# A transformer block on one core: first batch's norm on VectorE, ScalarE's steps interleaved, four part slots, and the last batch's chain in halves

## The chip, the cores and the metric

The kernel runs on one core of a Trainium2 chip. Five engines work side by side and meet at semaphores: TensorE (PE in the rows) for matrix products and transposes, VectorE (DVE), ScalarE (ACT), GpSimd (POOL), and SyncE (SP), which here only issues DMA transfers. Each engine runs its own instructions strictly in order. The metric is the device time of one execution in microseconds (us); less is better.

## The reference

The input x has 4 batches of 512 tokens of 128 channels. A small conditioning vector c per batch gives six modulation rows. The block is attention and then a mixture of experts, each behind a layer norm with modulation:

```python
mod = (_silu(L0_c) @ L0_wmod).reshape(4, 6, 1, -1)
sa, ca, ga, sb, cb, gb = (mod[:, i] for i in range(6))
ga = (2 * (ga >= 0) - 1) * jnp.maximum(jnp.abs(ga), 0.25)      # gb likewise
h = _layernorm(x) * (1 + ca) + sa
x = x + ga * attention(h)        # 16 heads of 8; q = h Wd Wu + rope(h Wd Wr), k likewise; softmax
h = _layernorm(x) * (1 + cb) + sb
x = x + gb * experts(h)          # sigmoid gates; each of 8 experts takes its 512 best tokens of 2048,
                                 # gelu(ex W1 + b1) W2 + b2, times the gate, added back
```

## The kernel before

There are three stretches. In the **head**, each batch b is normed (`moments`, `rstd`, `normed_1`), turned by TensorE (`turn_x`), scaled and shifted to hT by ScalarE (`h_out`) and projected (`project_k`, `project_rest`). VectorE adds bias and rotation (`rotate_k`, `parts_k`); the sum of a batch's keys is kf (L799). Keys and queries are then split into three bfloat16 parts each: high (a rounded copy, ScalarE's `key_high` and `query_high`), middle (`key_mid`, `query_mid`, of the first difference) and low (the second difference). VectorE forms the key differences, GpSimd the query sum (`rotate_q`, `parts_q`: L392, L398) and differences (L401, L405). SyncE stores each part to DRAM (`store_parts`) and reads them back in another layout (`load_group`). The part buffers kp and qp have two slots, used by batches in turn, so the high part of batch 3 waits until the stores of batch 1 are done (semaphores w_k, w_q).

The **attention** works on 16 groups (4 batches by 4 groups of heads). For each group TensorE computes the scores for the row maxima (`max_unit`, 8 a group, L1188), VectorE reduces each to maxima (`maxima`, L839, a semaphore count each), GpSimd splits the maxima in parts (`max_parts`) and SyncE moves them beside the queries (`load_max`, L295); then TensorE computes the scores again (`exp_unit`), ScalarE takes the exponential and TensorE weighs the values (`weigh`). Maxima run two groups ahead of the exponentials, so those of groups 0 and 1, all 16, stand before the first `step`. Beside them TensorE does the value products (`project_v`) and three of the four modulation rows (`modrows`).

After the last group comes the **tail** of batch 3: copy of the output (`out_copy`, L667), transposes (`out_turn`, L1238), division by the row sums (`normed`, L824 and L828), transposes (`turn_a`), copy (`a_out`), output projection (`project`), residual and statistics (`residual`, L855), rstd on GpSimd (L512), norm (`normed_2`, L875), transposes (`turn_h`, L1273), scale and shift (`h2_out`, L890), gate products (`route_gates`, L1284), exponential and reciprocal (`gates_out`, `gates_in`, L899). Each step takes the whole batch of four tiles of 128 tokens. `keep_warm(1)` puts one unused product of 512 columns between. Then VectorE searches the gates' thresholds, GpSimd gathers the rows of each expert, and the experts run.

The order on every engine is written out by hand. On ScalarE in the head it is all norms and h first, and then the parts:

```python
            for b in range(1, NB):
                normed_1(b)
                h_out(b)
            act.wait_ge(s_bd, 1)
            for b in range(NB):
                ...
                key_high(b, u)
```

## Time and profile before

| what | us |
|---|---|
| median of 3 runs | 424.71 (424.31 to 425.78) |
| profiled execution, its own time | 423.78 |
| its span, first to last instruction | 422.0 |
| PE busy in the span | 313.6 (74%) |
| DVE busy | 270.2 (64%) |
| ACT busy | 205.7 (49%) |
| POOL busy | 180.6 (43%) |

The times in the profile count from the first instruction of the span. In a timeline row the bracket at the end says how long the engine had been idle and who ended it. A row that merges several instructions says so with x and their number.

### The profile page before, as it was taken

The page shows a single profiled execution, that of the slowest core. Times are in us where ns is not written, and L with a number is a line of the kernel's source. Part 1 is how long each engine was busy: PE and PEld are TensorE (multiplying, and loading weights), DVE is VectorE, ACT ScalarE, POOL GpSimd, SP SyncE. Part 2 cuts the span into 40 slices and gives each one's busy share as a digit, 9 for nine tenths or more (in the row PEclk, how much of TensorE's full clock was granted, in tenths as well). Part 3 has the DMA queues.
Part 4 walks back from the last instruction along what each step waited for, and adds up shares of the span by engine and source line. Part 5 has one row for each costly group of instructions (what it writes and reads, how often), then busy time and mean ns, then how long its engine had stood idle before and what let it go on. Part 6 is the DMA issues. An engine that isn't in the chain of part 4 may idle for free.

```text
span 422.0 us, 7330 instructions
## 1 busy us (share of the span) xinstructions
PE 313.6 (74%) x2326; PEld 148.7 (35%) x2326; DVE 270.2 (64%) x540; ACT 205.7 (49%) x394; POOL 180.6 (43%) x208
## 2 busy tenths in 40 slices
PE   4998375999999999999989984101378996690930
PEld 3533042323333333333335333100244764460630
DVE  4459878898999999999976934677642442220210
ACT  2654232888888889888886550100033242211200
POOL 5237541666611111111113713000086877788672
PEclk9999679999999999999999998555587999966895
DMA  8322861011111111111002300700023565544332
GB/s 241 86 101 84 299 227 39 7 43 40 40 40 41 40 39 38 39 38 43 26 4 83 97 0 25 206 0 0 2 66 115 121 145 117 112 83 79 28 28 19
DMA packets 34488, 30.39 MB, mean 72 GB/s; under 512 B 5280, under 2 KB 28704, under 8 KB 34464
## 3 DMA queue, kind: packets, MB, share of 16 engines
q1 hardware_dynamic: 28320, 23.65, 18.2%
q0 software_dynamic: 6144, 6.43, 9.1%
q8 instruction: 14, 0.23, 0.2%
q14 instruction: 10, 0.08, 0.1%
HBM read 18.27 MB, written 11.60 MB: 71 GB/s over the span
## 4 chain that ended last, share of the span: by engine, by line
PE 44%; DVE 18%; POOL 16%; issue 10%; DMA 5%; ACT 4%; ACTq 0%; DVEq 0%; SPq 0%; POOLq 0%
PE ps L1225 14%; POOL out L558 10%; PE ps L1188 8%; PE ps L1211 6%; DVE mx L839 5%; POOL ex L547 5%; DVE big L954 3%; PE ps L1426 2%; DMA out<-big,idx 2%; PE ps L1238 2%; ACT osb L667 2%; DVE KB L875 1%; PE ps L1455 1%; DMA k_parts<-big 1%; PE ps L1306 1%
## 5 line engine op out<-in xcount | busy, mean ns | idle before, releaser
L839 DVE TENSOR_REDUCE mx<-ps 128x2 f32<-128x1024 f32 x128 | 148.2, 1218 | 10.0 <-PE ps L1188 10.0
L690 ACT ACTIVATE big<-ps 128x512 f32<-128x512 f32 x256 | 139.3, 598 | 26.5 <-PE ps L1211 24.5
L1225 PE MATMUL ps<-big,VA 128*32 128x256 f32 (+1 forms) x960 | 80.1, 405 | 3.0 <-ACT osb L667 2.3
L1188 PE MATMUL ps<-KB,QB 48*128 48x512 bf16 x256 | 50.6, 397 | 12.1 <-DVE mx L839 10.6
L547 POOL DMA_INDIRECT ex<-rows,idx x32 | 34.3, 1073 | 51.4 <-DVE idx L1058 40.8
L1211 PE MATMUL ps<-QB,KB 51*128 51x512 bf16 x256 | 54.7, 382 | 1.7 <-ACT osb L667 1.1
L558 POOL DMA_INDIRECT out<-big,idx x32 | 50.4, 1574 | 13.1 <-issue 8.8
L736 ACT ACTIVATE big<-ps,b1c 128x512 f32<-128x512 f32 x32 | 22.0, 687 | 66.2 <-PE ps L1426 66.2
L427 POOL TENSOR_TENSOR VA<-Vall,bv_row 128x128 f32 (+1 forms) x16 | 7.3, 454 | 72.2 <-PE ps L1225 72.2
L1426 PE MATMUL ps<-big,w1s 128*128 128x512 f32 x64 | 35.8, 680 | 2.0 <-DVE big L1024 1.6
L1455 PEld LDWEIGHTS ps<-w2s,big 128*128 128x128 f32 x256 | 30.3, 196 | 6.5 <-issue 4.7
L1188 PEld LDWEIGHTS ps<-KB,QB 48*128 48x128 bf16 x256 | 12.1, 93 | 57.0 <-DVE mx L839 31.0
L1225 PEld LDWEIGHTS ps<-big,VA 128*32 128x32 f32 x960 | 19.3, 107 | 36.5 <-issue 34.7
L1455 PE MATMUL ps<-w2s,big 128*128 128x128 f32 x256 | 31.0, 280 | 0.9 <-ACT big L736 0.9
L1211 PEld LDWEIGHTS ps<-QB,KB 51*128 51x128 bf16 x256 | 21.9, 94 | 14.7 <-ACT big L690 5.3
L1024 DVE COPY big<-ps 128x512 f32<-128x512 f32 x8 | 5.5, 692 | 33.3 <-PE ps L1415 33.3
L1069 DVE TENSOR_TENSOR big<-ps,b2r 128x256 f32<-128x256 f32 x16 | 6.8, 424 | 30.8 <-PE ps L1455 30.8
L1400 PE MATMUL ps<-big,same_e 128*128 128x3 f16 x15 | 2.8, 186 | 24.5 <-DVE big L954 24.5
L1415 PE MATMUL ps<-ident,ex 128*128 128x128 f32 x32 | 6.4, 335 | 19.4 <-DMA ex<-rows,idx 19.4
L437 POOL CAST mxp<-mxn 16x128 bf16<-16x128 f32 x16 | 4.5, 279 | 37.5 <-ACT mxn L660 19.7
L727 ACT ACTIVATE big<-ps 16x64 f32<-16x64 f32 (+1 forms) x2 | 0.5, 267 | 40.3 <-PE ps L1437 40.3
L1426 PEld LDWEIGHTS ps<-big,w1s 128*128 128x128 f32 x64 | 12.3, 218 | 14.6 <-issue 9.6
(172 smaller groups left out, 413.9 us busy)
## 6 DMA issues: line engine op xcount, KB each, us to landing
KB<-k_parts SPq DMA_DIRECT2D x32, 96.0 KB
QB<-q_parts SPq DMA_DIRECT2D x32, 96.0 KB
w1s<-in_w SPq DMA_DIRECT2D x8, 256.0 KB, 2.8
w2s<-in_w SPq DMA_DIRECT2D x8, 256.0 KB, 3.0
k_parts<-big SPq DMA_DIRECT2D x4, 384.0 KB, 3.2
q_parts<-big SPq DMA_DIRECT2D x4, 384.0 KB, 4.5
QB<-mxp SPq DMA_DIRECT2D x96, 2.0 KB
rows<-rw SPq DMA_DIRECT2D x1, 1088.0 KB, 6.0
```

Of the source, the lines that this page charges most:

```text
L547: pool.indirect_dma_start(out=ex[:, e % 2, c, :], out_offset=None, in_=rows_dram, in_offset=bass.IndirectOffsetOnAxis(ap=idx[:, e, c:c + 1 ...
L558: pool.indirect_dma_start(out=out_rows, out_offset=bass.IndirectOffsetOnAxis(ap=idx[:, e, c:c + 1], axis=0), in_=ys[:, e % 2, c, :], in_of ...
L667: nc.scalar.activation(osb[:], ps[:, 6, :], ACT.Copy).then_inc(s_oe, 1)
L690: nc.scalar.activation(PT[:, u, 2 * i + half, kc, :], ps[:, EXP_BANKS[n], :], ACT.Exp, scale=SCALE).then_inc(s_ex, 1)
L736: nc.scalar.activation(hid[:, u, f, :], ps[:, 1 + f, :], ACT.Gelu, bias=bias).then_inc(s_gelu, 1)
L839: nc.vector.tensor_reduce(mx[:, u, :].rearrange("p (h a) -> p h a", h=2)[:, :, n], ps[:, max_bank(u, n):max_bank(u, n) + 2, :], AX.X, ALU.max,
L954: ins = nc.vector.tensor_scalar(ge3[:, j, :], sv, now[:, j:j + 1].bitcast(fp32), None, ALU.is_ge, ALU.add, accum_out=cnt3[:, j:j + 1])
L1188: ins = mm(ps[:, max_bank(u, n) + half, :], QB[rows, r, i, qc * 128:(qc + 1) * 128], KB[rows, r, i, :], start=True, stop=True)
L1211: mm(ps[:, EXP_BANKS[n], :], KB[rows, r, i, kc * 128:(kc + 1) * 128], QB[rows, r, i, :], start=True, stop=True).then_inc(s_sc, 1)
L1225: ins = mm(ps[32 * j:32 * j + 32, 6, cols], VA[:, u, kc, j, :], PT[:, u, j, kc, cols], start=kc == 0 and not cols.start, stop=kc == TC - 1 ...
L1426: mm(ps[:, 1 + f, :], w1s[:, u, f * 128:(f + 1) * 128], exT[:, u, :], start=True, stop=True).then_inc(s_up, 1)
L1455: ins = mm(ps[:, 5 + h, at * 128:(at + 1) * 128], hid[:, u, f, c * 128:(c + 1) * 128], w2s[:, u, f, :], start=f == 0, stop=f == FC - 1)
```

## The change

In the head, GpSimd fills `ones` first, and TensorE begins with sixteen products of that tile that nobody reads. The norm of batch 0 moves from ScalarE to VectorE (it then needs no nmr). ScalarE's copies of the weight product stand behind the first `h_out`, and its norms and h of the later batches stand between the part steps of batches 0 and 1. On TensorE the bias products move behind the transposes of batch 0 and the first row product behind the key products; `project_rest(1)` goes ahead of `turn_x(3)`; the row and value products beside the maxima are issued in halves, one between each two units. kp and qp have a slot for each of the four batches, so ScalarE waits for no store; SyncE stores batch 1 before it loads group 1, and so on. GpSimd's and VectorE's loops over batches are written out.

In the tail, the chain of the last batch is issued in two halves of two tiles, with a pair of PSUM banks at each step, and sixteen unused products of 256 columns take the place of `keep_warm(1)`. The aggregate of the statistics, the epsilon, rstd and the last reciprocal stay whole.

The diff, cut; parts left out of the halves have the same pattern as those shown:

```diff
+LAST_O, LAST_A, LAST_GATES = (2, 4), (3, 5), (1, 7)
...
-        kp, qp = view(2, 3, L, dt=bf16), view(2, 3, L, dt=bf16)
+        kp, qp = view(NB, 3, L, dt=bf16), view(NB, 3, L, dt=bf16)
...
-            store_parts(0, 0)
-
+            store_parts(0)
             sp.wait_ge(s_one, 1)
-            sp.wait_ge(w_k[0], 16 + 48)
-            sp.wait_ge(w_q[0], 16 + 48)
+            sp.wait_ge(w_k[0], 48)
+            sp.wait_ge(w_q[0], 48)
             load_group(0, 0)
+            store_parts(1)
             load_group(0, 1)
-            store_parts(1, 1)
-            store_parts(2, 0)
+            store_parts(2)
             load_group(0, 2)
-            store_parts(3, 1)
+            store_parts(3)
             load_max(0, 0)
             load_group(0, 3)
-            for u in range(2):
-                sp.wait_ge(w_k[u], 16 + 96)
-                sp.wait_ge(w_q[u], 16 + 96)
+            for b in range(1, NB):
+                sp.wait_ge(w_k[b], 48)
+                sp.wait_ge(w_q[b], 48)
...
-                sp.wait_ge(s_x2, b + 1)
+                sp.wait_ge(s_x2, b + 1 if b + 1 < NB else NB + 1)
...
-            for s_ in (*w_k, *w_q):
-                pool.sem_inc(s_, 16)
+            nc.gpsimd.memset(ones[:], 1.0).then_inc(s_ones, 1)
...
+            rotate_q(0)
+            rounded_q(0)
+            low_q(0)
+            rotate_q(1)
+            for b in range(1, NB):
+                rounded_q(b)
+                if b + 1 < NB:
                     rotate_q(b + 1)
...
+            act.wait_ge(s_modc, 2)
+            h_out(0)
             act.wait_ge(s_wc, 1)
             nc.scalar.activation(wc[:, 0:512], ps[:, 6, :], ACT.Copy)
             nc.scalar.activation(wc[:, 512:640], ps[:, 7, 0:128], ACT.Copy).then_inc(s_wce, 1)
-            act.wait_ge(s_modc, 2)
-            normed_1(0)
-            h_out(0)
+            normed_1(1)
             modrow_out(0)
-            for b in range(1, NB):
-                normed_1(b)
-                h_out(b)
+            h_out(1)
+            normed_1(2)
             act.wait_ge(s_bd, 1)
-            for b in range(NB):
-                u = b % 2
-                key_high(b, u)
+            key_high(0)
+            query_straight(0)
+            key_mid(0)
+            query_high(0)
+            h_out(2)
+            normed_1(3)
+            query_mid(0)
+            key_high(1)
+            query_straight(1)
+            key_mid(1)
+            h_out(3)
+            query_high(1)
+            for b in range(2, NB):
...
-            out_copy(15)
-
-
-            gates_out(3)
+            act.wait_ge(s_pv, NS)
+            act.wait_ge(s_ot, NS - 1)
+            for h in range(2):
+                cols = slice(h * L // 2, (h + 1) * L // 2)
+                nc.scalar.activation(osb[:, cols], ps[:, 6, cols], ACT.Copy).then_inc(s_oe, 1)
+            for h in range(2):
+                cols = slice((3 * TC + 2 * h) * NE, (3 * TC + 2 * h + 2) * NE)
+                act.wait_ge(s_gl, NB + h)
+                ins = nc.scalar.activation(ge[:, cols], ps[:, LAST_GATES[h], cols], ACT.Exp, scale=-1.0)
+            ins.then_inc(s_ge, 1)
...
+            dve.wait_ge(s_rstd, 1)
+            for n in range(TC):
+                ins = nc.vector.tensor_scalar(xn[:, n, :], X[:, n, :], mv[:, n, 0:1], rstd[:, n:n + 1],
+                                              ALU.subtract, ALU.mult)
+            ins.then_inc(s_xn, 1)
...
-            normed(15, LAST_TURN)
-            a_out(3)
-            residual(3)
-            normed_2(3)
-            h2_out(3)
+            for h in range(2):
+                cols = slice(8 * h, 8 * h + 8)
+                dve.wait_ge(s_ot, NS + h)
+                o = ps[:, LAST_O[h], 0:L // 2].rearrange("p (a d) -> p a d", d=32)
+                nc.vector.reciprocal(rs[:, cols].unsqueeze(2), o[:, :, HD:HD + 1]).then_inc(s_rs, 1)
...
+            dve.wait_ge(s_y, NB - 2)
+            for h in range(2):
+                dve.wait_ge(s_aT, NB + h)
+                nc.vector.tensor_copy(aT[:, 1, h * L // 2:(h + 1) * L // 2],
+                                      ps[:, LAST_A[h], 0:L // 2]).then_inc(s_aTe, 1)
+            for h in range(2):
+                rows = slice(3 * TC + 2 * h, 3 * TC + 2 * h + 2)
+                dve.wait_ge(s_y, NB + h)
+                nc.vector.tensor_tensor(x2[:, rows], ps[:, LAST_GATES[h], 0:2 * D].rearrange("p (c d) -> p c d", c=2),
+                                        X[:, rows, :], ALU.add).then_inc(s_x2, 1)
+                dve.wait_ge(s_x2, NB + h)
+                for n in range(rows.start, rows.stop):
+                    ins = nc.vector.bn_stats(stat2[:, n, :], x2[:, n, :])
+                ins.then_inc(s_st2, 1)
...
+            for c in range(TC):
+                n = 3 * TC + c
+                ins = nc.vector.tensor_scalar(xn2[:, 1, c, :], x2[:, n, :], mv2[:, n, 0:1], rstd2[:, n:n + 1],
+                                              ALU.subtract, ALU.mult)
+                if c % 2 == 1:
+                    ins.then_inc(s_xn2, 1)
...
+            warm_x = ones[:].bitcast(bf16)
+
+            def stay_warm(n):
+
+                for _ in range(n):
+                    mm(ps[:, 6, 0:256], warm_x[:, 0:128], warm_x, start=True, stop=True)
+
+            pe.wait_ge(s_ones, 1)
+            stay_warm(16)
...
             turn_x(0)
-            modrows(0, 1)
+            for j in range(4):
+                mm(ps[:, 5, j:j + 1], w_ct[:, j * D:(j + 1) * D], bcol[:, 0:1], start=True, stop=True)
+            mm(ps[:, 5, 128:256], bcol[:, 0:1].to_broadcast([128, 128]), w_ct[:, 4 * D:5 * D],
+               start=True, stop=True).then_inc(s_bias, 1)
             pe.wait_ge(l_wx, 16)
             project_k(0)
+            modrows(0, 1)
             turn_x(1)
             pe.wait_ge(s_wce, 1)
             pe.wait_ge(s_modc, 2)
...
             project_rest(0)
             turn_x(2)
             project_k(1)
+            project_rest(1)
             turn_x(3)
-            project_rest(1)
             project_k(2)
...
-                if n == 2:
-                    pe.wait_ge(s_qt, NB + 1)
-                    modrows(1, 6)
-                if n == 4:
-                    project_v(0)
-                if n == 6:
-                    project_v(1)
+                if n in (1, 2):
+                    modrow_half(1, n - 1)
+                if n in (3, 4):
+                    project_v(0, n - 3)
+                if n in (5, 6):
+                    project_v(1, n - 5)
                 if n == 7:
-                    pe.wait_ge(s_modr, 2)
-                    modrows(2, 6)
+                    modrow_half(2, 0)
...
+                if n == 0:
+                    modrow_half(2, 1)
+                if n in (1, 2):
+                    project_v(2, n - 1)
+                if n in (3, 4):
+                    project_v(3, n - 3)
+                if n in (5, 6):
+                    modrow_half(3, n - 5)
...
-            out_turn(15, LAST_TURN)
-            turn_a(3)
-            project(3)
-            keep_warm(1)
-            turn_h(3)
-            route_gates(3)
...
+            pe.wait_ge(s_x2, NB - 1)
+            pe.wait_ge(s_ge, NB - 1)
+            for h in range(2):
+                pe.wait_ge(s_aTe, NB + h)
+                for c in range(2):
+                    at = (2 * h + c) * 128
+                    ins = mm(ps[:, LAST_GATES[h], c * 128:(c + 1) * 128], aT[:, 1, at:at + 128], wo_g[:, 3, :],
+                             start=True, stop=True)
+                ins.then_inc(s_y, 1)
+            stay_warm(16)
+            for h in range(2):
+                pe.wait_ge(s_xn2, NB + h)
+                for c in range(2):
+                    ins = nc.tensor.transpose(ps[:, LAST_A[h], c * 128:(c + 1) * 128], xn2[:, 1, 2 * h + c, :], ident[:])
+                ins.then_inc(s_h2t, 1)
+            pe.wait_ge(s_x2, NB + 1)
+            for h in range(2):
+                pe.wait_ge(s_h2e, NB + h)
+                for c in range(2 * h, 2 * h + 2):
+                    n = 3 * TC + c
+                    ins = mm(ps[:, LAST_GATES[h], n * NE:(n + 1) * NE], h2T[:, 1, c * 128:(c + 1) * 128], wg[:],
+                             start=True, stop=True)
+                ins.then_inc(s_gl, 1)
```

## Rows read from the trace of the kernel before

**Rows 1.** The page: the granted clock of TensorE in 40 slices, and one group of instructions.
```profile
PEclk9999679999999999999999998555587999966895
...
L1069 DVE TENSOR_TENSOR big<-ps,b2r 128x256 f32<-128x256 f32 x16 | 6.8, 424 | 30.8 <-PE ps L1455 30.8
```

**Rows 2.** The chain that ended last: start us, length us, what.
```profile
44.95 4.74 DMA k_parts<-big
...
67.03 4.63 DVE mx L839 x4
...
305.78 1.96 POOL ex L547
```

**Rows 3.** Timeline of the first 30 us: start us, us, engine, line, operation, idle before.
```profile
4.37 0.20 POOL L379 MEMSET ones<- 128x128 f32 x1
...
5.46 1.87 PE L1099 MATMUL ps<-se,wmod 128*128 128x4 f32 x8 [5.46 <-DVE se L753]
...
7.15 1.04 POOL L385 TENSOR_TENSOR rstd<-var,mhalf 128x4 f32<-128x4 f32 x1 [2.58 <-DVE var L767]
...
9.10 0.64 PE L1104 MATMUL ps<-w_ct,wdT 128*128 128x128 f32 x2
...
12.33 0.28 DVE L781 TENSOR_TENSOR bv_row<-bv_row,ps 128x128 f32<-128x128 f32 x1
...
13.32 0.78 ACT L599 ACTIVATE big<-ps,modcol 128x512 f32<-128x512 f32 x1 [1.27 <-PE ps L1125]
...
18.30 0.75 DVE L787 SCALAR_TENSOR_TENSOR big<-ps,bcol,cos_t 128x512 f32<-128x512 f32 x1 [5.70 <-PE ps L1133]
...
20.48 0.75 DVE L799 SCALAR_TENSOR_TENSOR big<-ps,bcol,big 128x512 f32<-128x512 f32 x1
```

**Rows 4.** Timeline from 30 to 62 us.
```profile
30.17 0.75 DVE L799 SCALAR_TENSOR_TENSOR big<-ps,bcol,big 128x512 f32<-128x512 f32 x1
...
33.93 1.16 POOL L405 TENSOR_TENSOR big<-big 128x512 bf16<-128x512 f32 x1
...
43.54 0.61 PE L1188 MATMUL ps<-KB,QB 48*128 48x512 bf16 x4 [1.24 <-DMA QB<-q_parts]
...
44.50 0.75 DVE L799 SCALAR_TENSOR_TENSOR big<-ps,bcol,big 128x512 f32<-128x512 f32 x1
...
46.48 2.35 DVE L839 TENSOR_REDUCE mx<-ps 128x2 f32<-128x1024 f32 x2
...
54.46 0.61 PE L1188 MATMUL ps<-KB,QB 48*128 48x512 bf16 x2 [3.55 <-DVE mx L839]
...
55.00 2.08 PE L1152 MATMUL ps<-wc,big 128*128 128x128 f32 x8
...
57.66 3.49 DVE L839 TENSOR_REDUCE mx<-ps 128x2 f32<-128x1024 f32 x3 [1.32 <-PE ps L1188]
```

**Rows 5.** Timeline from 62 to 100 us.
```profile
62.03 1.16 PE L1152 MATMUL ps<-wc,big 128*128 128x128 f32 x8
...
63.86 4.07 SPq L295 DMA_DIRECT2D QB<-mxp  x6
```

**Rows 6.** Timeline from 237 to 269 us.
```profile
237.26 4.18 DVE L875 TENSOR_SCALAR KB<-X,mv,rstd 128x128 f32<-128x128 f32 x4 [0.73 <-POOL rw L518]
...
251.16 0.60 ACT L667 ACTIVATE osb<-ps 128x512 f32<-128x512 f32 x1 [1.19 <-PE ps L1225]
...
255.78 0.69 DVE L855 TENSOR_TENSOR X<-ps,X 128x512 f32<-128x512 f32 x1 [1.25 <-PE ps L1261]
...
259.13 1.12 DVE L875 TENSOR_SCALAR KB<-X,mv,rstd 128x128 f32<-128x128 f32 x4 [1.13 <-POOL rstd L512]
...
260.30 1.11 PE L1273 MATMUL ps<-ident,KB 128*128 128x128 f32 x4 [3.70 <-DVE KB L875]
...
262.32 1.88 PE L1284 MATMUL ps<-wg,h2T 128*128 128x8 f32 x8 [0.90 <-DVE h2T L890]
...
264.68 0.35 DVE L899 RECIPROCAL g_en<-ge 128x32 f32<-128x32 f32 x1
```

More of the change, by code:

```diff
@@ L195, in build @@
         s_qh, s_qr, s_qm, s_ql = (sem(n) for n in ("s_qh", "s_qr", "s_qm", "s_ql"))
-        w_k = [sem(f"w_k{u}") for u in range(2)]
-        w_q = [sem(f"w_q{u}") for u in range(2)]
+        w_k = [sem(f"w_k{b}") for b in range(NB)]
+        w_q = [sem(f"w_q{b}") for b in range(NB)]
         s_one = sem("s_one")
@@ L392, in rotate_q, with rounded_q @@
                 nc.gpsimd.tensor_tensor(qad[:], qcs[:], qss[:], ALU.add).then_inc(s_qad, 1)
-            def parts_q(b, u, more=True):
+            def rounded_q(b):
                 pool.wait_ge(s_qad, b + 2)
@@ L514, in rows_2 @@
             def rows_2(b):
-                pool.wait_ge(s_xn2, b + 1)
+                pool.wait_ge(s_xn2, b + 1 if b + 1 < NB else NB + 1)
                 rows = rw[:, b * TC:(b + 1) * TC, 0:D]
@@ L652, in _ @@
             values_out(1)
-            modrow_out(2)
             def max_out(s):
@@ L693, in _ @@
             max_out(0)
+            modrow_out(2)
             values_out(2)
@@ L903, in _ @@
             rotate_k(0)
-            with dve.Fori(0, NB // 2 - 1) as it:
-                parts_k(it * 2, 0)
-                parts_k(it * 2 + 1, 1)
-            parts_k(NB - 2, 0)
-            parts_k(NB - 1, 1, more=False)
+            for b in range(NB):
+                parts_k(b, more=b + 1 < NB)
             for n in range(3, 8):
@@ new lines, in _ @@
+            dve.wait_ge(s_st2, 2 * NB)
+            for n in range(3 * TC, 4 * TC):
+                ins = nc.vector.bn_aggr(mv2[:, n, :], stat2[:, n, :])
+            ins.then_inc(s_st2, 1)
+            dve.wait_ge(s_st2, 2 * NB + 1)
+            nc.vector.tensor_scalar_add(var2[:, 3 * TC:], mv2[:, 3 * TC:, 1], EPS).then_inc(s_v2, 1)
+            dve.wait_ge(s_r2, NB)
+            dve.wait_ge(s_xm2, NB - 2)
+            dve.wait_ge(s_h2t, NB - 2)
+            for c in range(TC):
[4 more added lines that the diff above has]
+                    ins.then_inc(s_xn2, 1)
@@ L943, in _ @@
+            dve.wait_ge(s_gl, NB - 2)
+            for h in range(2):
+                cols = slice(h * L // 2, (h + 1) * L // 2)
+                dve.wait_ge(s_h2t, NB + h)
+                nc.vector.tensor_scalar(h2T[:, 1, cols], ps[:, LAST_A[h], 0:L // 2], modcol[:, 3, 3:4], modcol[:, 2, 3:4],
+                                        ALU.mult, ALU.add).then_inc(s_h2e, 1)
             gates_in(3)
@@ L1104, in _ @@
             mm(ps[:, 7, 0:D], wdT[:], w_ct[:, 512:640], start=True, stop=True).then_inc(s_wc, 1)
-            for j in range(4):
-                mm(ps[:, 5, j:j + 1], w_ct[:, j * D:(j + 1) * D], bcol[:, 0:1], start=True, stop=True)
-            mm(ps[:, 5, 128:256], bcol[:, 0:1].to_broadcast([128, 128]), w_ct[:, 4 * D:5 * D],
-               start=True, stop=True).then_inc(s_bias, 1)
             def modrows(b, bank):
@@ L1299, in beside_14 @@
                         stage(b)
-            warm_x = ones[:].bitcast(bf16)
-            def stay_warm(n):
-                for _ in range(n):
-                    mm(ps[:, 6, 0:256], warm_x[:, 0:128], warm_x, start=True, stop=True)
             def step(q, r, prev=True, prev2=True, more_max=True, turn=True, beside=None):
```

108 lines of the change are left out of this document (63 added, 45 removed).

## The prediction

> **What bounds the kernel now.** I began with the chain of work that ended last, then read the timeline of the two stretches that the change touches. The reader is to see three things.
>
> First, the head: until 71.65 the chain runs through VectorE, which must finish the 16 row maxima of the first two groups before the exponentials of group 0 can start [rows 2]. The loop over the groups that follows is not changed, so whatever the head gains or loses passes on undiminished.
>
> Second, VectorE in the head is not full. It idles 5.70 us before the first rotation of the keys [rows 3]; the low part of batch 0 cannot be formed until ScalarE, busy with the norms of batches 1 to 3, writes the first high part; and at batch 3 ScalarE waits to 49.7 for a store of an earlier batch to free its part slot: the 4.74 us stand in the chain [rows 2]. VectorE has two maxima to do under it, to 46.48+2.35 = 48.83 [rows 4], and goes on when the high part is written, some 0.7 after the store: 50.4, so 1.6 us lost.
>
> Third, the tail: from the last copy of group 15 (251.16) to the end of the last gates (264.68+0.35 = 265.03) each step waits for the one before on another engine, whole batch by whole batch; the last two TensorE steps run at half clock [rows 6]. The search for the threshold, the gathers and the experts follow and hang on this point alone, since the stores issued around it have some 40 us until the first gather of the chain at 305.78 [rows 2]. So 265.03 also shifts the end one for one.
>
> The sum is made against the profiled execution: span 422.0, own time 423.78. That time is 0.93 below the median 424.71; I subtract the gain from the median. 0.3%, about what a measurement can tell from no change, is 1.3 us.
>
> **The head, part by part.**
> *Warm-up.* `ones` is now filled first. Its fill ended at 4.57, behind the other fills [rows 3]; now TensorE can start at about 1.5. Sixteen 256-column products take 3.4 us as an estimate: a pair of 512-column products took 0.61 at half clock [rows 4], so a pair of 256 takes some 0.4. They end at about 5.0, before L1099's 5.46, so they cost nothing unless `ones` is 0.5 late. What they bring is the clock. From 5.46 to 18.2 TensorE's durations are those of the 1.2 GHz level (though the clock row shows no event yet), and in the maxima stage it went from the granted 0.5 at 55.00 (L1152 x8 in 2.08) to full at 62.03 (1.16, ratio 0.56) after some 4 us of dense products [rows 1, 4, 5]. By analogy I take full clock from about 8.
>
> *Norm of batch 0 on VectorE.* rstd is ready at 8.19. Four tensor_scalar of this size took 1.12 alone [rows 6] and 4.18 beside GpSimd's row work [rows 6]. GpSimd has nothing between 8.19 and the next pow, so 1.12: ready at 9.3. The Trainium skill ("SBUF — State Buffer", section "Who interferes with whom") says that VectorE and GpSimd share one port pair as an exclusive lock; the 4.18 agrees, and by it the sum would be the same here, because GpSimd is idle. The four ScalarE norms and their wait for the weight copies vanish, and the copies move behind h of batch 0: h ends at about 10.8 rather than 13.32+0.78 = 14.10 [rows 3].
>
> *First rotation.* TensorE now does transposes, the bias products (at most 2.6 before, 1.4 at 0.56) and the two key products (18.30-14.10 = 4.2 with the end of the row product; 3.4 alone, 1.9 at 0.56): ready at 13.3. VectorE is later: its moments of batches 1 to 3 are pushed by 1.5 and the bias sum (ended 12.61) ends at about 14.2 to 14.4. So the rotation starts at 14.4 instead of 18.30, gain 3.9; the row product and the transposes of batch 1 now stand before the straight part, which takes 0.2 back: **3.7** at the sum kf of batch 0 (L799, 20.48 before).
>
> *Woven ScalarE order.* From kf(0) to kf(1) took 30.17-20.48 = 9.69; from kf(1) to kf(3) 14.33, or 7.17 a batch [rows 3, 4]. The first was long because ScalarE wrote the high part of batch 0 only after all four h. Now that part comes 0.5 after kf(0), and I take a usual 7.17: gain **2.5**. Against it: h of batch 2 stands behind the high query part of batch 0, which waits for GpSimd. Working the chain through (query sum on GpSimd to 21.9, ScalarE to 22.6, h(2) to 23.4, norm(3) to 25.0, transposes, key products to 27.4) the rotation of batch 2 begins at 27.5 where VectorE would be free at 27.1: **-0.3**. kf(3) then lies at 38.6 (44.50 before), the first maximum at 40.6 (46.48 before).
>
> *Four slots.* The wait for a slot goes, and with it the 1.6 us of VectorE. It could not bind earlier than batch 3 here, so nothing more. What is late next is TensorE: from 46.48 to 61.15 VectorE had 8 maxima of 1.16 and two differences, 10.7; idle 4.0, so 2.4 besides the slot. The halved row and value products stand between all the units instead of whole ones after three of them. At half clock (TensorE idles before, as now) unit 0.61 plus half product 1.0 is 1.6 against 1.16: units 4 to 7 cost VectorE 0.4 to 0.6 each, 2.0 together, saving 0.4. Bounds: 0 idle (all hidden at full clock) to the 2.4 of before. Sum **2.0**: the first eight maxima end at 53.2. The second eight took 10.5 with 1.3 idle; I take 10.3, gain **0.2**.
>
> *DMA queue.* The parts of batch 0 are complete 8 us earlier; load (0,0) reached TensorE 43.54-35.09 = 8.4 after the last part was ready, so at about 35.5, before TensorE is done projecting. Stores of batch 1 now stand before load (0,1): their last part should be ready at about 35, six stores and four loads issue in some 7, and the load is wanted at 53. Hidden by 8 us. The maxima themselves need 63.86-61.15 = 2.7 to become parts, 4.07 to issue, some 2 to land [rows 5]: 53.2+8.8 = 62.0 against 63.5 when the exponentials can start. Hidden by 1.5, as before by 1.7.
>
> Head: 3.7+2.5-0.3+2.0+0.2 = **8.1**.
>
> **The tail.** A 256-column VectorE operation out of PSUM took 424 ns (page, L1069) where 512 columns took 0.69 [rows 1, 6], so two halves cost 0.85: the halves gain only by overlap. ScalarE's half copy is not in the trace: between 0.30 and 0.60; 0.37 by the same ratio. Step by step from 251.16: copies end 251.5 and 251.85; transposes of halves 251.95 and 252.3; reciprocal and product of each half on VectorE 0.48, so 252.5 and 253.0 (253.09 before: nothing won yet); transposes 252.85 and 253.35; copies 253.4 and 253.85; output projection 254.05 and 254.5 (255.74 before); x2 and statistics of both halves on VectorE, 4 x 0.43 with gaps, 255.9 (257.37 before: 1.5 won); aggregate, eps, pow unchanged 1.75: 257.65; norm 1.12 with the first half out at 258.25; transposes, scale-and-shift and gates of half 0 lie under those of half 1, of which remain 0.35, 0.45, 0.55; exponential 0.2, gates 0.6: 261.1. Before 265.03: 3.9 if TensorE keeps 2.4 GHz, which sixteen small products to about 257 instead of one pair to 256.5 should do. At 1.2 GHz (the 1.11 and 1.88 of L1273, L1284) the halves left are 0.6 and 0.95: 261.8, gain 3.2. Bounds 3.2 and 3.9; every semaphore hop is doubled, so I take **3.5**.
>
> Sum 8.1+3.5 = 11.6: span 410.4, own time 412.2, median 424.71-11.6 = **413.1**.
>
> **Rivals.**
> *Cold start* (0.22). The first warm-up ends and L1099 and the wait for weights follow, sparse for 2 us; before, TensorE was at work from 5.46 and stayed at 1.2 GHz to 18.2. Then TensorE is free at 9.74, the key products end at 16.4, kf(0) comes at about 19. Gain 1.5 instead of 3.7: total 9.4, **415.3**. The rows of the start [rows 3] speak for it, those of the maxima [rows 4, 5] against it. The Trainium skill ("TensorE: Matmul & The Clock Gate", section "What's actually happening") says that sustained activity lifts the clock at a point that need not follow the first product by a fixed time; the late rise and the quick one in this trace agree.
> *ScalarE's new order holds VectorE up* (0.15). ScalarE takes its steps in order; each wait for GpSimd now also delays a norm or h. If batches 2 and 3 each lose 1.7, 3.4 is gone: **416.5**. For it: the batches keep 7.17 although VectorE's eight operations of 0.7 fill only 5.6, so something else already paces them; against it: h(2) is late by only 0.3 in my working.
> *More* (0.10). The clock stays at 2.4 GHz through the maxima: 2 of the idle 2.0 plus 1 in group 0's step gone: **410.2**.
> *Slower* (0.02). Load (0,1) now waits behind six stores, the last of which needs the low query part of batch 1. The load took 8.4 with all that lies before it, so it decides from about 45 on; slower than before by 1.3 only if that part comes after 45+11.6+1.3 = 58, against the 35 worked out. One such collision would give **426**.
> *The head does nothing* (0.01): only 3.5, **421.2**; the profile speaks against it, since 5.70 and 1.6 idle are plain.
>
> **How the numbers follow.** Likeliest 0.50, own range 411.5 to 414.8 (tail 3.2 to 3.9, maxima idle 0.5 to 2.4, first rotation within 1). The range takes in the cold start and the held-up order with their spread, and the better case: 409.9 to 417.2, leaving out under 0.2. Faster 0.96, same 0.01, slower 0.03 (the last case and what I cannot see).
>
> **What the profile after would show.** The norm of batch 0 on VectorE at 8.2 to 9.3; first rotation near 14.4 (16.5 and later: cold start); L799's successor at about 16.8, 24, 31.4, 38.6 (later from the third on: held-up order); no ScalarE wait on k_parts; first maximum at 40.6, eighth ends at 53.2, sixteenth at 63.5; last gates at 257.0 (265.03-8.1) less 3.5 = 253.4. It would be wrong most if the maxima were held by TensorE at half clock or by load (0,1).

## The result, and the profile after

The change makes the kernel faster, by about half of what was forecast: 421.67 us (median of 20 runs, 418.46 to 424.98) beside 426.52 for the kernel before (20 runs, 424.31 to 428.25), ratio 0.987, 95% interval 0.985 to 0.989. Forecast was 413.1 against 424.71, a ratio of 0.973. The profiled execution after has a span of 420.1 (own time 421.91), the one before 422.0 (423.78). That one was quick for its kernel: 2.7 below the median of these 20 runs, so the pair of profiles shows less gain than the timing.

The head starts as planned and then waits for TensorE. Timeline of the kernel after, rows of VectorE, TensorE and ScalarE in the first 20 us:

```profile
3.78 1.27 PE L1159 MATMUL ps<-ones 128*128 128x256 bf16 x5
5.48 1.06 PE L1165 MATMUL ps<-se,wmod 128*128 128x4 f32 x8 [0.42 <-DVE se L767]
7.30 1.12 PE L1169 MATMUL ps<-w_ct,wdT 128*128 128x512 f32 x2 [0.77 <-DMA bcol<-in_bcol]
8.26 1.12 DVE L791 TENSOR_SCALAR big<-X,mv,rstd 128x128 f32<-128x128 f32 x4 [1.10 <-POOL rstd L382]
9.53 1.09 PE L1186 MATMUL ps<-ident,big 128*128 128x128 f32 x4 [0.88 <-DVE big L791]
...
12.54 1.91 PE L1193 MATMUL ps<-big,w_x 128*128 128x512 f32 x2
14.25 1.72 PE L1194 MATMUL ps<-big,w_x 128*128 128x512 f32 x2
...
16.08 0.75 DVE L806 SCALAR_TENSOR_TENSOR big<-ps,bcol,cos_t 128x512 f32<-128x512 f32 x1 [2.04 <-PE ps L1194]
...
16.86 0.60 ACT L588 ACTIVATE modrow<-ps 128x512 f32<-128x512 f32 x1 [2.88 <-PE ps L1173]
...
17.60 0.63 PE L1186 MATMUL ps<-ident,big 128*128 128x128 f32 x4 [0.78 <-ACT modrow L588]
...
19.20 0.75 DVE L818 SCALAR_TENSOR_TENSOR big<-ps,bcol,big 128x512 f32<-128x512 f32 x1 [0.98 <-PE ps L1199]
```

L791 is the moved norm: 1.12 us, as forecast. But a key product of two times 512 columns takes 1.91 (1.02 at the full clock, e7 below), and the first rotation comes at 16.08 instead of 14.4. The warm-up was spent: L1169 still runs at the full clock, L1186 no more. From the rotation to the sum kf it then takes 3.12 us, against 2.18 before [rows 3] and 2.4 forecast. TensorE cannot turn batch 1 before ScalarE has copied the row product (L588), whose product the change moved to just before that step, and the straight part (L1199) stands behind. In e7, where the clock is full, the same stretch takes 3.11.

The sum kf (L818) follows at 26.51, 34.16 and 41.33; ScalarE waits for no part slot. The maxima start at 43.31 (46.48 before [rows 4]) and then run at 1.69 us each, not 1.16. TensorE in that stage, kernel after:

```profile
43.45 1.22 PE L1224 MATMUL ps<-wmod,se 128*128 128x256 f32 x2 [3.70 <-DVE big L825]
44.60 0.61 PE L1265 MATMUL ps<-KB,QB 48*128 48x512 bf16 x2
...
51.01 0.61 PE L1265 MATMUL ps<-KB,QB 48*128 48x512 bf16 x2
51.55 1.22 PE L1213 MATMUL ps<-wc,big 128*128 128x128 f32 x4
52.70 0.61 PE L1265 MATMUL ps<-KB,QB 48*128 48x512 bf16 x2
53.24 1.22 PE L1213 MATMUL ps<-wc,big 128*128 128x128 f32 x4
54.39 0.61 PE L1265 MATMUL ps<-KB,QB 48*128 48x512 bf16 x2
```

The same stage by windows of 2 us (busy us of each engine, then the granted clock, the DMA share and GB/s), kernel after:

```profile
50.00:52.00 2.00, 2.00 (x8) 1.34 (x9) 1.54 (x2) 1.22 (x3) 1.15 (x1) 0.50 0.31 110
52.00:54.00 2.00, 2.00 (x9) 1.34 (x9) 1.53 (x2) 0.00 (x0) 0.00 (x0) 0.50 0.90 294
...
60.00:62.00 2.00, 2.00 (x9) 1.14 (x8) 1.51 (x2) 0.10 (x1) 0.00 (x0) 0.50 0.02 3
```

And VectorE, kernel after, its group of maxima from 43 to 77 us, and then the last maximum of the first eight, the first of the second eight and the 16th in the timeline:

```profile
L858 DVE TENSOR_REDUCE mx<-ps 128x2 f32<-128x1024 f32 x19 | 23.2, 1224 | 9.4 <-PE ps L1265 9.4
```

```profile
55.04 1.23 DVE L858 TENSOR_REDUCE mx<-ps 128x2 f32<-128x1024 f32 x1 [0.47 <-PE ps L1265]
57.37 1.23 DVE L858 TENSOR_REDUCE mx<-ps 128x2 f32<-128x1024 f32 x1 [1.10 <-PE ps L1265]
...
69.46 1.23 DVE L858 TENSOR_REDUCE mx<-ps 128x2 f32<-128x1024 f32 x1 [0.47 <-PE ps L1265]
```

The reader is to see that TensorE has no gap from 50 to 56 and stays at 0.50: a pair of score products and a half product start every 1.69 us, and VectorE, which needs 1.16 to 1.23 for each, idles 9.4 us over 15 waits. Before, the clock had returned to full at about 59 [rows 1, 5] and the last eleven of the 16 maxima ran in three blocks at VectorE's own pace. After, it returns at about 77. So the 8th maximum ends at 56.27 (61.15 before), the 16th at 70.69 (71.65 before), the copy L717 that begins the tail stands at 251.36 (251.16 before [rows 6]). In this pair of profiles the head's whole lead is gone.

The tail, kernel after:

```profile
251.36 0.66 ACT L717 ACTIVATE osb<-ps 128x256 f32<-128x256 f32 x2 [1.19 <-PE ps L1302]
...
255.39 3.18 PE L1159 MATMUL ps<-ones 128*128 128x256 bf16 x16
...
260.87 1.26 POOL L521 TENSOR_TENSOR rw<-rw,modrow 128x512 f32<-128x512 f32 x1
...
261.52 0.65 DVE L916 TENSOR_SCALAR ge<-ge 128x32 f32<-128x32 f32 x1 [0.98 <-ACT ge L721]
262.21 0.35 DVE L918 RECIPROCAL g_en<-ge 128x32 f32<-128x32 f32 x1
```

From the copy to the end of the gates 11.20 us against 13.87 before [rows 6]: 2.67 gained of the 3.5 forecast. An addition of 32 columns takes 0.65 because GpSimd's L521 runs beside it; it takes 0.18 where L521 is over (e3) or comes later (e8).

### The profile page after: what moved, and what is told of

It reads as the page before. It is cut to its first block, busy times and chain, and to the rows that moved or that the text cites. A ratio compares the mean times of both kernels' runs of the same rounds, so it can differ in the third digit from the quotient of the medians.

```text
span 420.1 us, 7394 instructions
## 1 busy us (share of the span) xinstructions
PE 324.8 (77%) x2362; PEld 155.6 (37%) x2362; DVE 272.4 (65%) x549; ACT 204.4 (49%) x392; POOL 180.6 (43%) x207
## 4 chain that ended last, share of the span: by engine, by line
PE 47%; DVE 17%; POOL 17%; issue 10%; ACT 4%; DMA 3%; ACTq 0%; DVEq 0%; SPq 0%; POOLq 0%
PE ps L1302 14%; POOL out L559 10%; PE ps L1265 10%; PE ps L1288 6%; POOL ex L548 5%; DVE mx L858 3%; DVE big L1011 3%; PE ps L1527 3%; PE ps L1315 2%; ACT osb L674 2%; PE ps L1213 2%; DMA out<-big,idx 2%; PE ps L1556 1%; DVE KB L894 1%; PE ps L1159 1%
## 5 line engine op out<-in xcount | busy, mean ns | idle before, releaser
L548 POOL DMA_INDIRECT ex<-rows,idx x32 | 34.2, 1070 | 51.6 <-DVE idx L1115 40.8
L559 POOL DMA_INDIRECT out<-big,idx x32 | 50.5, 1579 | 13.3 <-issue 8.8
L1265 PE MATMUL ps<-KB,QB 48*128 48x512 bf16 x256 | 53.5, 415 | 2.7 <-DVE mx L858 2.6
L741 ACT ACTIVATE big<-ps 16x64 f32<-16x64 f32 (+1 forms) x2 | 0.5, 266 | 40.8 <-PE ps L1538 40.8
```

The lines of the kernel that those rows point to most:

```text
L548: pool.indirect_dma_start(out=ex[:, e % 2, c, :], out_offset=None, in_=rows_dram, in_offset=bass.IndirectOffsetOnAxis(ap=idx[:, e, c:c + 1 ...
L559: pool.indirect_dma_start(out=out_rows, out_offset=bass.IndirectOffsetOnAxis(ap=idx[:, e, c:c + 1], axis=0), in_=ys[:, e % 2, c, :], in_of ...
L1265: ins = mm(ps[:, max_bank(u, n) + half, :], QB[rows, r, i, qc * 128:(qc + 1) * 128], KB[rows, r, i, :], start=True, stop=True)
```

## The experiments

Theory A: TensorE at half clock all through the 16 maxima takes the head's gain back, and the halved row and value products keep it there. Rival B: the halves' handovers hold TensorE up at any clock. Ratios are to the kernel before, run beside each kernel. The runs were made in four groups on four chips, and the medians of before were 431.79 (e1 to e4), 426.02 (e5 to e8), 431.65 (e9 to e12) and 426.50 (f1 to f3), so only ratios and profiles are compared between groups. In the profiles the difference between the chips lies behind the first gather: from there to the first write of an expert's rows (L559) it is 25 us in f1 and 31 in e4. What comes before it can be compared.

**e1, the head alone; e2, the tail alone.** e1 has the last batch's chain of the kernel before; e2 is the kernel before with the new chain.

> The head of the change with the tail of before. Both theories say: what is missing against the whole change is the tail's gain, 2.5 to 3 us (2.7 in the two profiles, from the last copy to the gates). Theory A (TensorE stays at 1.2 GHz through the 16 maxima and so takes back what the earlier start gained): the head is worth only 1 to 5 us against before, from execution to execution, with the maxima at 1.69 us each while the clock is low. Rival B (the halves of the products with their handovers hold TensorE up at any clock): 1.69 us each at either clock, and little spread.

> The tail of the change with the head of before. Expected 2.5 to 3 us faster than before (ratio 0.993 to 0.994), with the same spread as before; if the two parts hinder each other the sum of this and of the head alone differs from the whole change by more than 1 us.

Measured: e1 0.9984 (0.9955 to 1.0014), e2 0.9958 (0.9935 to 0.9981). In e1 the maxima begin at 43.45 and the 16th ends at 70.82; in e2 at 46.82 and 73.07. The head is 3.4 us ahead when the maxima begin and 2.2 when they end. The tail in e2 takes 11.16, as after. Two small parts, then, and the head's is the one that missed. They do not add up to the whole: 0.16% and 0.42% against 1.3% (after, and e4 beside them), some 3 us apart, somewhat more than the intervals explain. Some 0.9 us of it shows in the profile of e1: its old tail takes 14.79 instead of 13.87, the output projection running at half clock (2.08 instead of 1.16 us). So what the new tail gains depends on the clock as well. The rest of the 3 us stays open.

**e3, whole products.**

```diff
-                if n in (3, 4):
-                    project_v(0, n - 3)
+                if n == 4:
+                    project_v(0, 0)
+                    project_v(0, 1)
...
```

The other halves are joined in the same way, at their places in the kernel before.

> The whole change, but the row and value products beside the maxima are issued whole again, after units 2, 4, 6, 7 and 1, 3, 5, as before. Theory A: TensorE works denser after a whole product and idles between, the clock rises within the maxima as it did in the profile of before (near 59), the sixteenth maximum ends at about 66 to 68 instead of 70.7 and the time is 2 to 4 us below the whole change. Rival B as well says faster, but then by the pace of each unit at half clock already. If the halves were right, this is slower by 1 to 2 us.

Measured: 0.9802 (0.9768 to 0.9836). TensorE's clock is 1.00 from 55, the 16th maximum ends at 66.89 instead of 70.69 and the copy L717 comes at 246.59, 4.8 earlier than after. The halves cost, then, and were no gain. Rival B forecast a gain here too, so e3 does not decide between them.

**e4, the wait before the maxima filled** with 24 unused products of 256 columns.

> The whole change, and 24 unused products of 256 columns before the first maxima unit, where TensorE sat idle from 39.8 to 43.5. Theory A: the clock stays at 2.4 GHz through the maxima, each takes 1.2 us, the sixteenth ends at 62 to 63 instead of 70.7, and the time falls by 6 to 8 us against the profile of the change (median about 414 to 415). Rival B: the maxima keep 1.69 us and the time does not move.

Measured: 0.9871 (0.9846 to 0.9896), as after. The clock was full up to 45, was 0.57 in 45 to 50 and then 0.50: it fell within the maxima. Theory A had forecast 62 to 63 for the 16th maximum, and that failed: it ends at 70.22. TensorE's idle 3.7 us before the maxima is not the cause by itself. As the clock was low again, e4 does not speak for rival B either.

**e5, halves kept, TensorE filled beside them.**

```diff
+                if n >= 2:
+                    for _ in range(3):
+                        mm(ps[:, 7, 0:256], warm_x[:, 0:128], warm_x, start=True, stop=True)
```

> The kernel after, with three more unused products of 256 columns, in a PSUM bank that is free, after each of the units 2 to 7 of the first eight maxima; the row and value products stay in halves. TensorE gets 0.33 us of work more a unit at the full clock, 0.66 at half of it. Theory A (the half products spread TensorE's work so thin that its clock stays at 0.50 all through the 16 maxima, and this clock is what eats the head's gain): the clock rises within the maxima, some units are 2.3 us long before it does, the 16th maximum ends between 66 and 69 us instead of 70.7 and the ratio to the kernel before falls from 0.987 to between 0.980 and 0.984. Rival B (the handovers of the halves between TensorE and the engines that empty their banks hold it up at any clock): the clock may rise, but the 16th maximum ends at 71 or later, 0.987 or above. A third: the clock doesn't rise for the fillers, each unit costs 0.66 more, the 16th ends at 74 or later, 0.993.

Measured: 0.9799 (0.976 to 0.9839). TensorE in e5; L1410 are the unused products:

```profile
46.88 0.61 PE L1265 MATMUL ps<-KB,QB 48*128 48x512 bf16 x2
47.42 1.22 PE L1213 MATMUL ps<-wc,big 128*128 128x128 f32 x4
48.44 0.85 PE L1410 MATMUL ps<-ones 128*128 128x256 bf16 x3
49.27 0.55 PE L1265 MATMUL ps<-KB,QB 48*128 48x512 bf16 x2
49.75 0.71 PE L1213 MATMUL ps<-wc,big 128*128 128x128 f32 x4
50.30 0.49 PE L1410 MATMUL ps<-ones 128*128 128x256 bf16 x3
50.72 0.39 PE L1265 MATMUL ps<-KB,QB 48*128 48x512 bf16 x2
...
60.42 0.39 PE L1265 MATMUL ps<-KB,QB 48*128 48x512 bf16 x2 [1.20 <-DVE mx L858]
```

and VectorE in e5:

```profile
49.86 5.10 DVE L858 TENSOR_REDUCE mx<-ps 128x2 f32<-128x1024 f32 x4 [0.65 <-PE ps L1265]
55.74 4.62 DVE L858 TENSOR_REDUCE mx<-ps 128x2 f32<-128x1024 f32 x4 [0.78 <-PE ps L1265]
60.85 4.62 DVE L858 TENSOR_REDUCE mx<-ps 128x2 f32<-128x1024 f32 x4 [0.49 <-PE ps L1265]
```

With more work to do, TensorE gets its full clock at 49.6 and every product is done in 0.6 of the time. From 55 on nothing is added any more, TensorE even waits for VectorE (60.42), and the clock stays full to 66. The maxima come in blocks of four at 1.155 us each, and the 16th ends at 65.47, 5.2 earlier than after, and a little better than theory A forecast (66 to 69, 0.980 to 0.984). Theory A stands; rival B falls, since the same halves with the same handovers keep VectorE busy. The twenty executions of after point the same way, if weakly: the six quickest (418.46 to 419.29) had a mean granted clock of 0.865 to 0.869, and all but one of the others 0.845 to 0.864.

**e10, the control: the same unused products in e2**, the kernel with the old head and the new tail.

> Control for e5: the kernel before with the new tail and the same 3 unused products behind units 2 to 7 of the first eight maxima. If the gain of e5 were the fillers' alone and the new head worth nothing, this kernel would gain the same 0.7% over e2_tail_only and come to 0.980 as e5 does. If the head is worth its 3.5 us once TensorE has its full clock (theory A), the first maximum stays at 46.8, the 16th ends at 69 to 72 us, and the ratio is 0.988 to 0.995.

Measured: 0.9978 (0.9959 to 0.9997), 16th maximum at 73.41, the tail's copy at 253.61. The fillers do nothing for the old head; its clock is 0.50 from 48 to 60 with them too. With the new one (e5) the copy stands at 244.98. With the same fillers the new head is thus worth 8.6 us in the profiles and 1.8% in the ratios: 2.7 by the sum kf of batch 3, 5.2 in the maxima, 0.7 behind them. A part of the 5.2 is again the clock, which the fillers raise at 49.6 in e5 and at 60 in e10.

**e6, e3 and e4 together.**

> Whole products as in e3_whole_products, and the 24 unused products in TensorE's idle wait before the first maximum as in e4_fill_the_wait. Theory A: the clock is at its full rate when the maxima begin and the whole products keep it there, so the eight first maxima end at 53 to 54 us (e3: 56.4), the 16th between 63.5 and 65.5 (e3: 66.9), the ratio is 0.973 to 0.978 (e3: 0.980). If the clock falls inside the first maxima all the same, as in e4, it rises again where it does in e3, and the ratio is 0.979 to 0.982.

Measured: 0.978 (0.974 to 0.982); clock 0.68 in 45 to 50, 16th maximum at 66.57. By the profile it is the second case: as in e4 the full clock was lost once more inside the first maxima. The ratio lies between the two cases.

**e7, unused products in the early gaps; e8, all of it**: e6, e7, and GpSimd's scaling of the last rows moved behind the gates. One of the three places of e7:

```diff
+            for _ in range(6):
+                mm(ps[:, 3, 0:256], warm_x[:, 0:128], warm_x, start=True, stop=True)
             pe.wait_ge(l_id, 16)
             turn_x(0)
```

> The kernel after, with unused products in TensorE's gaps between 6 and 12 us: 5 before the folded weights' product, 6 before the first transposes, 10 before the first key product. Theory: TensorE's clock fell at 9.2 us for those gaps and cost the first batch's transposes and products 1 to 2 us, so the first rotation starts at 14 to 15 us instead of 16.1 and everything to the last first rotation is that much earlier (last key rounding starts at 39.3 to 40.3 instead of 41.3); as the maxima remain at half clock, the ratio falls by the same 1 to 2 us: 0.982 to 0.985. Rival: the first batch's path is set by its waits for VectorE and ScalarE, not by TensorE's clock: first rotation not before 15.8, ratio 0.987.

> Whole products, the filled wait, the early fillers, and in the tail GpSimd's scaling of the last batch's rows moved behind the gates, so that nothing of it runs beside the last gates' addition. If the terms add: e6's gain, 1 to 2 us from the early fillers and 0.5 us from the addition: ratio 0.968 to 0.974. If the early fillers only move a wait, 0.974 to 0.978.

Measured: e7 0.9888 (0.985 to 0.993), e8 0.9814 (0.9775 to 0.985). The profile of e7 has the full clock up to 40 us:

```profile
9.41 0.63 PE L1188 MATMUL ps<-ident,big 128*128 128x128 f32 x4 [0.31 <-DVE big L791]
...
12.09 1.02 PE L1195 MATMUL ps<-big,w_x 128*128 128x512 f32 x2
12.95 1.02 PE L1196 MATMUL ps<-big,w_x 128*128 128x512 f32 x2
...
14.09 0.75 DVE L806 SCALAR_TENSOR_TENSOR big<-ps,bcol,cos_t 128x512 f32<-128x512 f32 x1 [0.17 <-PE ps L1196]
```

The first rotation at 14.09 and everything to the 16th maximum (68.70) is 2.0 earlier than after. But that execution was the quickest of its six (418.8, the others to 422.2), and in the profile of e8 the same fillers lost the clock at 8.2 and the rotation came at 15.75. The early gain is there in one profile and not in the other; in the ratio it does not show. e8 missed both of its cases (0.974 to 0.978 was the worse). In e8 and e9 the addition before the gates takes 0.18, and the tail 10.70 and 10.68. But the 0.5 us come back behind the gates, in the search for the threshold. Timelines of f3, with the move, and of f1, without:

```profile
258.11 1.26 POOL L521 TENSOR_TENSOR rw<-rw,modrow 128x512 f32<-128x512 f32 x1
...
258.43 0.97 DVE L1028 TENSOR_TENSOR big<-cand_t,big 128x4 f32<-128x4 int32 x1
```

```profile
265.06 0.16 DVE L1028 TENSOR_TENSOR big<-cand_t,big 128x4 f32<-128x4 int32 x1
```

GpSimd's L521 now meets another small operation of VectorE. From the end of the gates to the first gather it is 41.3 us in e8, 41.3 in e9 and 41.2 in f3, against 40.8 in after, e5, e6 and f1. The move only shifts the collision.

**e9, unused products wherever the clock was seen to fall.**

> The kernel after with unused products wherever TensorE's clock was seen to fall: 20 instead of 16 at the start, 8 and 8 and 12 in the gaps between 6 and 12 us, 24 in the wait before the first maximum, 8 before and 8 behind the second unit, 5 behind the third, 3 behind units 3 to 7, 8 before the second row of maxima is turned; and GpSimd's scaling of the last batch's rows behind the gates. Halves kept. Theory A: full clock from the start to the tail, first rotation at 14.1 to 14.4 us (as in e7), first maximum at 41.3, the 16th maximum ends at 62 to 63.5 us instead of 65.5 in e5 and 70.7 after, ratio 0.967 to 0.973. If the clock is not held by them in most executions (e8's early fillers held it only from 11.6 on), the ratio is 0.976 to 0.980 as in e5 and e6.

Measured: 0.9751 (0.9728 to 0.9774); first rotation 15.02, 16th maximum 65.88, the tail's copy at 244.19. The timing lies between its two cases: the clock was 1.00 up to 50, then 0.55 to 0.60 up to 54. The first rotation is later than the 14.1 to 14.4 forecast although the early durations are those of the full clock; TensorE reaches the key products at 13.02 (12.09 in e7), with more fillers in front of them and 0.49 of waiting for a load.

**e11, two part slots in e5.**

```diff
                 act.wait_ge(s_kf, b + 2)
-                nc.scalar.activation(kp[:, b, 0, :], kf[:], ACT.Copy).then_inc(s_kh, 1)
+                if b >= 2:
+                    act.wait_ge(w_k[b - 2], 48)
+                nc.scalar.activation(kp[:, b % 2, 0, :], kf[:], ACT.Copy).then_inc(s_kh, 1)
...
```

The queries' parts are treated in the same way; the new order of ScalarE and of the queue stays.

> e5_halves_filled with two part slots instead of four (the new order of ScalarE and of the queue kept): ScalarE must again wait for the stores of batch 0 before it rounds batch 2's key, and for those of batch 1 before batch 3's. The prediction put woven order and slots together at 2.2 us. If the slots are a real part of the head's gain: ScalarE waits for k_parts before the key rounding of batch 2 or 3 by 1 to 4 us, the 16th maximum ends 1 to 4 us later than e5's 65.5, ratio 0.982 to 0.990. Rival: with the stores now issued earlier the slots are free in time, no wait, ratio 0.980.

Measured: 0.9804 (0.9773 to 0.9834). ScalarE's group of key roundings between 17 and 50 us:

```profile
L612 ACT ACTIVATE big<-big 128x512 bf16<-128x512 f32 x4 | 2.5, 623 | 2.3 <-DVE big L822 1.3 <-DMA k_parts<-big 1.0
```

In e10, with the old order, that wait is 5.8. With the new order two slots cost one wait of 1.0, and from the last kf to the 16th maximum it is 24.03 against 24.19 in e5. The stores come early enough without the two more slots; the gain is that of the order, ScalarE's and the queue's together.

**e12, after without its warm-up.**

> The kernel after without the 16 unused products at the start. The warm-up holds the full clock only to about 9 us in most profiles, and the first batch's products run at half clock all the same. Theory: only the products between 5 and 9 us lose, TensorE's clock is 0.50 up to about 16 us, the first rotation moves by less than 0.5 us, ratio 0.986 to 0.989 as after. Rival: without it the clock rises later than 16 us and the second batch's products are slow too: first maximum 1 us or more later.

Measured: 0.9919 (0.9899 to 0.994). In its profile L1168 takes 2.08 (half clock), but from 10.4 the durations are those of the full clock, and the first rotation comes at 13.78, ahead of every kernel with the warm-up. Neither case came true: the rotation is 2.3 earlier than after, and yet the ratio is worse. Near 243 the same profile has eight weighing products in 1.93 instead of 1.06, half clock for some 2 us, which costs 1.5.

**f1, f2, f3: after, e9 without its warm-up, and e9 with a filled tail, side by side.**

> The kernel after, unchanged, beside f2 and f3 on one chip. Ratio 0.985 to 0.989 as first measured. Its profile is one more look at TensorE's clock at the start: if the fall from 9 to 16 us belongs to the warm-up, the first rotation starts at 15.8 to 16.4 us again; if it is chance, somewhere between 13.8 and 16.4.

> e9_best without its 20 starting products; the fillers in the gaps between 6 and 12 us stay. If the warm-up is worth nothing or does harm: first rotation at 13.8 to 14.4 us, ratio 0.972 to 0.976, no worse than e9. If the warm-up is worth what e12 lost in the timing: ratio 0.979 to 0.983.

> e9_best with the last batch's chain filled too: 5 unused products behind the transposes of the attention's output, 5 behind those of the normed output, 28 instead of 16 behind the output products. If the tail's missing 0.3 us is TensorE's clock: from the copy of the attention's output to the end of the gates 10.2 to 10.5 us instead of 10.7 (e9) and 11.2 (after), ratio 0.973 to 0.975. If the fillers run into the chain instead: 10.8 or more, 0.976 or more.

Measured: f1 0.9896 (0.9881 to 0.9912), f2 0.9745 (0.9732 to 0.9759), f3 0.9729 (0.971 to 0.9749). f1's first rotation comes at 16.43, 0.35 later than in after, and its ratio is just above the 0.985 to 0.989 forecast. In f2 it comes late, at 18.04, against both cases, since the cold TensorE had the gap fillers to do, yet its clock is full from 13 to the end of the maxima and these take 24.04 from the last kf (25.61 in e9). By the ratio it is as fast as e9, although it starts 3 us behind. The tail of f3 takes 10.68, that of e9 10.68: filling gains nothing where the clock is full anyway, and the length lies between its two cases, 10.2 to 10.5 and 10.8. It is not always full: in e3, e6 and e7 TensorE idled 2.04 us for the norm and did the last gate products at half clock, 1.85 instead of 1.03, and the tail took 11.5 although GpSimd's L521 came too early to meet the addition (0.18). f3 has 28 products in that wait and 1.03. But e9 idled 2.04 us there too and still took 1.03, so the idle wait alone does not decide it. f3 is the fastest version, 415.51 beside 426.50.

## Why the prediction missed

**What failed: the clock in the maxima.** The step is "At half clock ... unit 0.61 plus half product 1.0 is 1.6 against 1.16: units 4 to 7 cost VectorE 0.4 to 0.6 each". The price was right, 1.69 measured. The number of units was not: all of them down to the 16th and into the first step, not four. The term that failed is thus the second eight, which I put at 10.3 us ("took 10.5 with 1.3 idle; I take 10.3"): they end 14.42 after the first eight, 4.1 too late, where the first eight are only 0.3 too late against kf. I had the rise at 55 to 62 from the kernel before and did not ask whether the halves leave it in place. They do not, and the same work in whole products does (e3); what about the whole products raises the clock is not shown. From the last kf to the end of the 16th maximum the forecast had 24.9, after has 29.36, and e5, with the clock, 24.19: 4.5 us. The step (0,0) behind them is at half clock up to 77 us, in e5 only from 67 to 70: from the 16th maximum to the tail's copy 180.67 against 179.51 in e5, 1.2 us.

**What failed next: full clock from about 8.** The warm-up lifted the clock and it fell again at 8.8, before the products it was meant for. kf(0) came at 19.20 instead of 16.8, 2.4 late. Of this 1.7 is the rotation (16.08 instead of 14.4), the clock's part: with the clock held (e7) it came at 14.09. The other 0.7 has another cause: the row product and its copy, which TensorE now has to wait for, cost 0.9 behind the rotation, and I had put 0.2. They cost as much at the full clock (e7), where kf(0) came at 17.20. My rival *cold start* named this place, and kf at "about 19" is what came; but it priced only this, at 415.3, and left the maxima alone. The place was right, the price partly luck, since 0.7 of it has the other cause. The Trainium skill ("TensorE: Matmul & The Clock Gate", section "What's actually happening") says that the number of cold products varies from run to run; the first rotation at 14.09 in e7 and 15.75 in e8 under the same fillers agrees. So do after and f1, one kernel: the eight small products behind the warm-up (L1165) took 1.06 in the one and 1.87, half clock, in the other.

**Right:** the norm on VectorE (8.26 to 9.38). **The woven order:** kf came every 7.4 us (forecast 7.27), with 0.3 more for the three steps together, so the rival *ScalarE's new order holds VectorE up* is out. **The slots:** the wait went, but two slots in the new order do as well (e11). **Loads:** no maximum or exponential waited for the moved loads.

**Mis-sized: the tail.** 2.67 instead of 3.5. Of the 0.83, 0.47 is the addition beside GpSimd's L521: GpSimd starts its two operations as early as the norm's end, and the faster chain now meets the second. The Trainium skill ("SBUF — State Buffer", section "Who interferes with whom") has VectorE and GpSimd exclude each other on a shared port pair; 0.65 beside 0.18 agrees. The move in e8, e9 and f3 takes it out of the tail and into the search, where it costs as much. Leaving the collision out, the tail gains 3.2 (10.68 in e9 and f3). That this is my lower bound is chance: the bound was worked out for half clock, and in e9 and f3 the last products ran at the full clock, for which I had 3.9. At half clock the gain was 2.4 (e3, e6, e7). So the steps themselves were priced 0.7 to 0.8 too low at either clock. In f3 the statistics of both halves end 5.18 us after the copy begins, where I had 4.74, and the other 0.3 comes behind them; that it is the doubled handovers was not tested.

Together at the end of the gates (forecast 253.4, after 262.56): 2.4 + 0.3 + 4.5 + 1.2 + 0.8 = 9.2 us in this execution. The timed miss is smaller, 0.014 of 425 or 6 us, because the profiled execution before, the base of the sum, was itself a quick one: e2 and e10 have the same head, and their tail's copy stands at 253.7 and 253.6, not at 251.16. With the clock looked after (f3, ratio 0.9729) the kernel gives the forecast ratio (0.973), but not by the forecast's terms: its gates end at 256.52, 3.1 behind 253.4, and the ratio is met because before usually takes 2.7 more than the profile that I started from. e5 says by which mechanism the greater part was missed.

**Open:** what decides TensorE's clock at the start, and whether the warm-up is worth having. Of the twelve profiles with it, six had full-clock durations behind it and lost them before 10 us (after, e1, e4, e5, e6, e8), two kept them (e7, e9), and in four (e3, e11, f1, f3) the products from 5 us on took the time of half clock. e12 says it is worth 0.2% to 0.5% in time (0.9919 against 0.9869 and 0.9896 on other chips), its profile says the contrary, and f2 against f3 differ by less than their intervals. One profile shows one execution. Nor did I try the norm on VectorE by itself, or the halves of the tail step by step; their shares are read from the rows alone. Why head and tail gain more together than apart is open too.

## What to carry to other kernels

Filler work cut fine so that it fits between the steps of another engine can leave TensorE at half clock where the same work in whole pieces lets the clock rise; check the clock of the stage after the change, not before it, and count how many units a slow clock would cover. Where a stage hangs on TensorE at 0.50, add work to it as an experiment: if the stage gets shorter, the clock was the limit. When an operation is moved out of the way of another engine, measure to a point behind both, not only to the end of the stage that it left. And compare the profiled execution with the median of more runs before its times become the base of a sum.

## What the hardware showed unexpectedly

- TensorE with 2.00 busy of 2.00 us stayed at 0.50 from 50 to 56 and again from 58 to 62, on pairs of 48-row score products and half products of four-byte numbers; with three more products of 256 columns and 128 rows per unit the clock went full 3.5 us after the first of them (e5, 46.10 to 49.6). A busy share of 100% in the trace is not the same as a clock that rises. What counts is not shown.
- Once full, the clock survived a gap of 1.20 us in the same stage (e5, 60.42); it fell at about 67, after one of 2.05 (before 65.73).
- The clock row and the durations disagree at the start: in e3 the row says 1.00 from 8 to 16 us, and the key products take 1.91 there (1.02 at the full clock). Durations of one known shape are the better witness. The Trainium skill ("TensorE: Matmul & The Clock Gate", section "Seeing it yourself") warns that clock events in traces can be unreliable; for the first 16 us this case agrees.
- An isolated fall of the clock in the middle of dense work (e12, 0.61 and 0.54 in 242 to 246) cost 1.5 us.
- GpSimd's 512-column operation made small operations of VectorE beside it several times longer: 0.65 instead of 0.18 (L916, after and e8), 0.97 instead of 0.16 (L1028, f3 and f1).
